# Reordering the attention steps of a fused attention and mixture-of-experts kernel

## Chip, cores and metric

One core of one Trainium2 chip. The metric is the device time of one execution in microseconds (us), as the median over runs. Engines are named as in the profile: PE is TensorE (PEld its weight load), DVE VectorE, ACT ScalarE, POOL GpSimd, SP SyncE, which here only issues DMAs.

## The reference, cut to what matters

```python
# x: (4, 512, 512); 16 heads of 32
h = layernorm(x)
q, k, v = split(h @ w_qkv)
q, k = layernorm_per_head(rope(q)), layernorm_per_head(rope(k))
a = tril((q @ k.T) ** 4)
x = x + ((a / a.sum(-1)) @ v) @ w_out
h = layernorm(x)
# 16 experts, 4 groups: the 2 best groups, in them the 4 best experts of each token,
# weights normalised and scaled by 2.5
x = x + sum_over_chosen(w_e * expert_e(h)) + shared_expert(h)
```

## The kernel before

Each engine has its own instruction stream, written out by hand, and semaphores between them. The part that the change touches is the attention of the four batches (`B = 4`, 512 tokens in `MB = 4` pieces of 128). A batch b is a sequence of 16 steps, `i = 4 m + p`: group m of four heads (`HG`), key piece p. Behind it come the projection with `w_out` and the residual (lines 559 and 1445), then the next batch. After the last batch come 96 expert tiles (some 590 us), which the change leaves alone.

A step has, on PE, `scores(b, i)` (L533: 12 matmuls in four banks, one for each head, the query width 512 - 128 p), then `fill`, then `values(b, i - 1)` (L548: 16 matmuls that add up values and row sums over the four key pieces of a group in banks 6 and 7), then `fill_behind`. The fills are work for the batch after (nb = b + 1), the one after that (lb = b + 2) and the one before (pb = b - 1), and they share two PSUM banks, bkA and bkB: q, k and v products of nb (L485, 8 matmuls for one of the three over one 128-token piece), transposes of its q and k (L494), of the first norm (L473) and of the second norm's rows (L473), the router's logits (L500), `places` (L510, L511) and `table` (L519).

ACT squares the scores of each head (`square`, L910), squares two of the four once more (`fourth`, L903; DVE does the other two in `fourths`, L1420), and splits a piece of an expert weight into two f16 parts (`split_next`, L819 and L821). POOL multiplies the diagonal block of each head by the causal mask (L1065) and computes the low f16 part (L1073). `scores(b, i + 1)` waits for the squares of step i, `values(b, i)` for the masks of step i, and the squares of step i + 1 for the second squares of step i.

- `finish(b, m)` on DVE (L1357 to L1363) reads banks 6 and 7 when the last `values` of group m is done, and divides. `values(b, 4 m + 4)`, the first of the next group, waits for it (`att_done`). Before, it stands ahead of the `fourths` of step 4 m + 5.
- `qkT` on ACT (L852, L856, two times each) empties both banks of q and k transposes, which PE writes at the end of steps 3, 7, 11 and 15. Before, the q half stands ahead of the next step's squares and the k half behind the second of them. PE's v product in the next step waits for the q half.
- `copy_v` (L878) empties the v product. Before, it stands at the start of step 4 m + 1, behind `split_next`. PE's q product of step 4 m + 1 waits for it. For batches from 2 on, its first one (m = 1, group step 4 or 5) also waits for `xn2_out`, the end of a 1 MB DMA that stores the second norm's rows of batch pb, because these rows lie in the same SBUF memory.
- `head_squares`, `head_variance`, `head_deviation`, `head_normed` (L882 ACT, L1403 DVE, L886 ACT, L1407 and L1411 DVE) are one chain for the norm of q and k; `centre` (L1393 to L1399, DVE) is ahead of it.
- SP issues in one queue: `store_half(n)` waits for the low part of piece n, which is done at the end of every second step; a store and a load of 768 KB follow. The row store (L380) waits for `xn16_ready`, which comes from `rows_lo` (L1425) in step 2, and stands behind the pieces of steps 1 and 3.
- Routing of batch pb on DVE, one serial chain of small operations: `group_sums`, `group_choice`, `compare`, `expert_choice` (which releases `places`), `choice_weights`, `choice_values`, `choice_places` (which releases the bank for the last q and k transposes), `place_rows` (L1328, L1329).

## Time and profile before

| | |
|---|---|
| median of 3 runs | 1217.14 us (1215.68 to 1225.99) |
| profiled execution | 1209.58 us, span 1207.6 us |
| mean granted TensorE clock | 0.905 of 2.4 GHz |
| busy share of the span | PE 79%, DVE 63%, ACT 47%, POOL 44% |
| attention steps of batches 0, 1, 2, 3 | 104.1, 134.6, 124.5, 94.9 us |

The difference between 1209.58 and 1207.6 us is what lies before the first and behind the last instruction. A timeline row has start, duration, engine, line, operation, what it writes and reads, how many instructions are merged in it, and in brackets how long its engine sat idle before it and which engine and line ended that. A group's duration is from the first start to the last end.

### The profile page before, as it was taken

The page shows a single profiled execution, that of the slowest core. Times are in us where ns is not written, and L with a number is a line of the kernel's source. Part 1 is how long each engine was busy: PE and PEld are TensorE (multiplying, and loading weights), DVE is VectorE, ACT ScalarE, POOL GpSimd, SP SyncE. Part 2 cuts the span into 40 slices and gives each one's busy share as a digit, 9 for nine tenths or more (in the row PEclk, how much of TensorE's full clock was granted, in tenths as well). Part 3 has the DMA queues.
Part 4 walks back from the last instruction along what each step waited for, and adds up shares of the span by engine and source line. Part 5 has one row for each costly group of instructions (what it writes and reads, how often), then busy time and mean ns, then how long its engine had stood idle before and what let it go on. Part 6 is the DMA issues. An engine that isn't in the chain of part 4 may idle for free. (4 is left out here: it accounts for less than half of the span.)

```text
span 1207.6 us, 21002 instructions
## 1 busy us (share of the span) xinstructions
PE 958.4 (79%) x5770; PEld 455.7 (38%) x5771; DVE 756.9 (63%) x1663; ACT 563.6 (47%) x1009; POOL 529.1 (44%) x738
## 2 busy tenths in 40 slices
PE   5967789869777785984777799888888798878883
PEld 2432333324333332341343454444344344434441
DVE  2857865867888588849648665554455544545552
ACT  2347874866537665577235234333333233333330
POOL 0005663544415545367302003555555555555553
PEclk9988999888879887976868899899999989999996
DMA  8002333433323333655346896777777777778874
GB/s 330 13 35 93 118 105 137 140 119 112 107 88 100 137 107 110 236 204 192 107 148 207 304 319 184 193 185 184 174 188 191 178 179 181 190 174 193 183 187 78
DMA packets 76648, 193.48 MB, mean 160 GB/s; under 512 B 9904, under 2 KB 11056, under 8 KB 75312
## 3 DMA queue, kind: packets, MB, share of 16 engines
q1 hardware_dynamic: 58672, 149.53, 35.9%
q0 software_dynamic: 17920, 43.26, 19.6%
q8 instruction: 28, 0.46, 0.1%
q14 instruction: 28, 0.23, 0.1%
HBM read 131.67 MB, written 61.10 MB: 160 GB/s over the span
## 5 line engine op out<-in xcount | busy, mean ns | idle before, releaser
L743 PE MATMUL bank<-arena,xgT 128*128 (+1 forms) x1152 | 288.0, 387 | 3.6 <-ACT xgT L1029 3.1
L1065 POOL TENSOR_TENSOR s_p<-s_p,c_causal 128x128 f32<-128x128 f32 x256 | 153.8, 624 | 304.3 <-DVE s_p L1420 282.7
L485 PE MATMUL bank<-arena 128*128 128x512 f32 x384 | 196.5, 663 | 43.8 <-ACT arena L856 14.6
L1022 ACT ACTIVATE hT<-bank 128x512 f16<-128x512 f16 x96 | 57.3, 597 | 273.1 <-PE bank L753 273.1
L743 PEld LDWEIGHTS bank<-arena,xgT 128*128 128x128 f16 x1152 | 109.2, 100 | 133.1 <-issue 45.4
L1073 POOL TENSOR_TENSOR arena<-arena 128x768 f16<-128x768 f32 x68 | 113.0, 1662 | 87.8 <-ACT arena L821 87.7
L1109 POOL DMA_INDIRECT out<-yy,sidx x80 | 128.6, 1608 | 46.1 <-issue 44.6
L764 PE MATMUL bank<-wd,hT 128*128 128x512 f16 x576 | 146.0, 391 | 0.7 <-ACT hT L1022 0.7
L910 ACT ACTIVATE arena<-bank 128x512 f32<-128x512 f32 (+3 forms) x256 | 100.8, 439 | 93.2 <-PE bank L533 92.6
L1694 DVE TENSOR_SCALAR yy<-bank,hsc 128x512 f32<-128x512 f32 x80 | 60.0, 750 | 122.8 <-DMA out<-yy,sidx 116.6
L1029 ACT ACTIVATE xgT<-bank 128x1024 f16<-128x1024 f16 x96 | 98.2, 1023 | 78.7 <-PE bank L734 77.4
L485 PEld LDWEIGHTS bank<-arena 128*128 128x128 f32 x384 | 78.3, 213 | 146.0 <-issue 93.0
L1420 DVE TENSOR_TENSOR s_p<-arena 128x512 f32<-128x512 f32 (+3 forms) x128 | 69.0, 558 | 73.5 <-ACT arena L910 72.3
L734 PE MATMUL bank<-ident,xg 128*128 128x128 f16 x768 | 61.1, 224 | 63.1 <-DMA xg<-xn_scratch,gidx 62.9
L1103 POOL DMA_INDIRECT xg<-xn_scratch,gidx x80 | 86.7, 1084 | 40.6 <-issue 39.1
L1654 DVE TENSOR_TENSOR hh<-sg,bank 128x256 f32<-128x256 f32 x96 | 40.4, 421 | 80.8 <-ACT sg L1038 79.5
L734 PEld LDWEIGHTS bank<-ident,xg 128*128 128x128 f16 x768 | 47.5, 100 | 102.5 <-DMA xg<-xn_scratch,gidx 94.6
L764 PEld LDWEIGHTS bank<-wd,hT 128*128 128x128 f16 x576 | 53.5, 100 | 49.6 <-issue 4.9
L1090 POOL COPY wr<-xg 128x1 f32 x80 | 60.2, 752 | 13.3 <-PE bank L734 10.3
L533 PE MATMUL bank<-arena 32*128 32x512 f16 (+3 forms) x768 | 50.1, 319 | 18.6 <-ACT arena L910 13.6
L548 PE MATMUL bank<-s_p,arena 128*32 128x512 f32 (+3 forms) x256 | 40.0, 523 | 28.9 <-DVE arena L1363 22.5
L903 ACT ACTIVATE s_p<-arena 128x512 f32<-128x512 f32 (+3 forms) x128 | 60.9, 476 | 2.0
(172 smaller groups left out, 1390.2 us busy)
## 6 DMA issues: line engine op xcount, KB each, us to landing
wd<-w_scratch SPq DMA_DIRECT2D x82, 512.0 KB, 4.2
arena<-w_experts SPq DMA_DIRECT2D x34, 768.0 KB, 6.0
w_scratch<-arena SPq DMA_DIRECT2D x34, 768.0 KB, 4.5
arena<-w_scratch SPq DMA_DIRECT2D x17, 1024.0 KB, 7.7
xin<-x SPq DMA_DIRECT2D x4, 1024.0 KB, 5.5
arena<-x SPq DMA_DIRECT2D x4, 1024.0 KB, 4.8
x_scratch<-arena SPq DMA_DIRECT2D x4, 1024.0 KB, 5.2
xg<-xn_scratch SPq DMA_DIRECT2D x16, 256.0 KB, 4.5
```

The lines of the kernel that those rows point to most:

```text
L485: mm = pe.matmul(bk[:], xnT[:, c, m * P:m * P + P], wqkv[:, c, w * E:w * E + E], start=(c == 0), stop=(c == EC - 1))
L734: mm = pe.transpose(oct16(bank[k])[:, c], xg[:, k, 0:E].bitcast(F16)[:, c * P:c * P + P], ident16[:])
L743: mm = pe.matmul(bank[2 + k][:], xgT[:, k, xh * EC + c, :], w, start=(c == 0 and xh + wh == 0), stop=(c == EC - 1 and xh == 1))
L764: mm = pe.matmul(bank[5 + k][:], hT[:, k, hh_ * FC + c, :], wd[:, k, wh, c, :], start=(c == 0 and hh_ + wh == 0), stop=(c == FC - 1 and hh ...
L903: act.activation(s_p4[:, i % 2, j, 0:w], s_sq[:, j, 0:w], ACT.Square).then_inc(p4_done[1], 1)
L910: act.activation(s_sq[:, j, 0:w], bank[j][:, 0:w], ACT.Square, scale=1.0 / (QS * QS)).then_inc(sq_done, 1)
L1029: act.activation(xgT[:, k], oct16(bank[k]), ACT.Copy).then_inc(gT_sb, 1)
L1065: pool.tensor_tensor(d, d, C["causal"][:], ALU.mult).then_inc(p4_masked, 1)
L1073: pool.tensor_tensor(halves[:, j, 1, a], stage[:, j, a], halves[:, j, 0, a], ALU.subtract).then_inc(lo_done, 1)
L1103: pool.indirect_dma_start(out=xg[:, k], out_offset=None, in_=xn_dram, in_offset=bass.IndirectOffsetOnAxis(ap=gidx[:, k:k + 1], axis=0)).th ...
L1109: pool.indirect_dma_start(out=out, out_offset=bass.IndirectOffsetOnAxis(ap=sidx[:, k:k + 1], axis=0), in_=yy[:, k], in_offset=None, comput ...
L1420: dve.tensor_tensor(s_p4[:, i % 2, j, 0:N - P * kb], s2, s2, ALU.mult).then_inc(p4_done[0], 1)
```

## The change

- PE: `values(b, i - 1)` goes ahead of `fill(b, i)` in the steps where i is 4, 8 or 12. In the last batch, the logits' 32 matmuls are spread over steps 5 and 6, two token pieces in each.
- DVE: `finish(b, m)` goes from ahead of the `fourths` of step 4 m + 5 to behind the `fourths` of step 4 m + 4, ahead of `split_qk`, `head_variance` and all else of that step. In the last batch likewise, and there `group_sums`, `group_choice` and `compare` each come one step later (7, 8 and 9, the last one together with `expert_choice`). In step 15, `choice_places` goes ahead of `centre`.
- ACT: all PSUM copies stand at the end of the step in which PE fills the bank, `qkT` in one piece there; `copy_v` of steps 4, 8 and 12 ahead of `split_next`, and `head_squares` from between the squares to behind `copy_v`. `copy_rows(3)` comes ahead of the first norm's activations in step 6. In the last batch `copy_logits` stands in step 7 instead of 6.
- SP: the row store stands behind one piece instead of two.

```diff
-                halves_of(b, 0, 2)
+                halves_of(b, 0, 1)
                 if b:
                     sp.wait_ge(xn16_ready, b)
                     sp.dma_start(xn_dram[N * (b - 1):N * b, 0:E]...).then_inc(xn2_out, 16)
-                halves_of(b, 2, 4)
+                halves_of(b, 1, 4)
...
-                elif i == 5:
-                    for m in range(MB):
+                elif i in (5, 6):
+                    pe.wait_ge(x2T_sb, upto(pb, 3))
+                    for m in (2 * i - 10, 2 * i - 9):
                         logits(pb, m, bkA)
...
                     scores(b, i)
+                    if i and i % MB == 0:
+                        values(b, i - 1)
                     if b + 1 < B:
                         fill(b, i)
-                    if i:
+                    if i % MB:
                         values(b, i - 1)
...
+            def behind(b, i):
+                nb, pb, lb, m, p = b + 1, b - 1, b + 2, i // MB, i % MB
+                if p == 3:
+                    qkT(nb, m, bkA, bkB)
+                elif i == 0 and b:
+                    copy_first(nb, 3, bkA)
+                elif i == 4 and b:
+                    copy_rows(pb, 1, bkB)
+                elif i == 5 and b:
+                    copy_rows(pb, 2, bkB)
+                elif i == 6 and b:
+                    copy_rows(pb, 3, bkA)
+                elif i == 8 and b:
+                    copy_logits(pb, bkB)
+                    gate_scores(pb)
+                elif i == 9:
                     copy_v(nb, 0, bkB)
...
-                    if nb < B and p == 0:
-                        if m:
-                            qkT(nb, m - 1, bkA, bkB, (1,))
-                        head_squares(nb, m)
                     square(b, i, 2)
                     fourth(b, i, 1)
                     square(b, i, 3)
                     fourth(b, i, 3)
+                    if nb < B and p == 0:
+                        if m:
+                            copy_v(nb, m, bkA)
+                        head_squares(nb, m)
                     if i == 2 and b:
                         rows_hi(b - 1)
                     split_next(b, i)
+                    if nb < B:
+                        behind(b, i)
...
-                if p == 1 and m:
-                    finish(b, m - 1)
-                elif p == 2 and (m < MB - 1 or lb < B):
+                if p == 2 and (m < MB - 1 or lb < B):
...
                 if p == 0:
                     if m:
+                        finish(b, m - 1)
                         split_qk(nb, m - 1)
                     head_variance(nb, m)
                 elif p == 1:
                     head_normed(nb, m)
-                elif p == 3 and (m < MB - 1 or lb < B):
+                if i == 15 and b:
+                    choice_places(pb, bkA)
+                if p == 3 and (m < MB - 1 or lb < B):
                     centre(nb if m < MB - 1 else lb, (m + 1) % MB)
...
-                        if i % MB == 1 and i > 1:
+                        fourths(b, i)
+                        if i and i % MB == 0:
                             finish(b, i // MB - 1)
-                        fourths(b, i)
                         last_behind(b, i)
```

## Rows read from the trace of the kernel before

**Rows 1.** Busy time by stretch: the 16 steps of batches 0 to 3.
```profile
core 0: us, PE busy (x) PEld busy (x) DVE busy (x) ACT busy (x) POOL busy (x), PEclk, DMA share, GB/s
88.91:192.99 104.08, 84.32 (x589) 33.87 (x589) 77.88 (x118) 80.80 (x162) 64.89 (x80) 0.93 0.31 107
...
206.92:341.51 134.59, 102.22 (x658) 45.46 (x657) 103.65 (x176) 89.78 (x177) 65.63 (x80) 0.84 0.36 123
...
356.32:480.83 124.51, 91.14 (x662) 41.59 (x661) 94.79 (x156) 85.12 (x169) 64.28 (x80) 0.86 0.34 115
...
495.95:590.84 94.89, 63.86 (x546) 27.99 (x545) 73.87 (x142) 67.39 (x141) 62.83 (x80) 0.77 0.58 206
```

**Rows 2.** Waits of PE in 88 to 592 us: total, times, longest.
```profile
PE bank L548 <- DVE arena L1363: 34.9, 6, 11.0
PE bank L485 <- ACT arena L856: 14.6, 7, 3.2
...
PE bank L485 <- ACT arena L878: 11.5, 6, 5.9
PE bank L485 <- ACT vtok L878: 9.2, 3, 7.9
PE bank L494 <- DVE rb L1295: 8.9, 2, 5.9
```

**Rows 3.** Timeline of PE in batch 2: steps 4, 5 and 13.
```profile
385.89 3.70 PE L485 MATMUL bank<-arena 128*128 128x512 f32 x8 [1.77 <-ACT arena L856]
...
397.26 5.71 PE L485 MATMUL bank<-arena 128*128 128x512 f32 x8 [5.91 <-ACT arena L878]
...
466.33 1.94 PE L548 MATMUL bank<-s_p,vtok 128*32 128x512 f32 x8 [10.97 <-DVE arena L1363]
```

**Rows 4.** Timeline of ACT: first value copy of batches 1 and 2.
```profile
247.36 0.60 ACT L878 ACTIVATE vtok<-bank 128x512 f32<-128x512 f32 x1 [5.71 <-DMA xn_scratch<-vtok]
...
396.61 0.60 ACT L878 ACTIVATE arena<-bank 128x512 f32<-128x512 f32 x1 [3.75 <-DMA xn_scratch<-arena]
```

**Rows 5.** Timeline of SP's queue in batch 1, the row store.
```profile
236.75 0.97 SPq L380 DMA_DIRECT2D xn_scratch<-vtok  x1
```

**Rows 6.** DMA issues in 200 to 600 us: KB each, median us to landing.
```profile
x_scratch<-arena SPq DMA_DIRECT2D x3, 1024.0 KB, 5.4
```

**Rows 7.** Timeline of DVE in batch 2: rows' low part, a finish, the ranks.
```profile
376.07 2.79 DVE L1425 SCALAR_TENSOR_TENSOR arena<-arena 128x512 f16<-128x512 f32 x4 [0.79 <-ACT arena L895]
...
393.10 0.70 DVE L1357 STREAM_TRANSPOSE arena<-bank 128x512 f32<-128x512 f32 x1
...
457.17 2.56 DVE L1219 TENSOR_TENSOR rb<-rb,c_tie 128x1024 f32<-128x1024 f32 x1
```

**Rows 8.** Timeline of ACT in batch 2, from the q and k copies to the split.
```profile
384.41 0.76 ACT L852 ACTIVATE arena<-bank,ln_b,ln_s 128x512 f16<-128x512 f32 x1
...
392.02 0.84 ACT L821 ACTIVATE arena<-arena 128x768 f32<-128x768 f32 x1
```

**Rows 9.** Timeline of POOL in batch 2, masks of step 3.
```profile
382.33 2.73 POOL L1065 TENSOR_TENSOR s_p<-s_p,c_causal 128x128 f32<-128x128 f32 x4 [1.39 <-DVE s_p L1420]
```

**Rows 10.** Timeline of DVE in batch 1, from step 10 to the finish.
```profile
290.69 0.76 DVE L1420 TENSOR_TENSOR s_p<-arena 128x256 f32<-128x256 f32 x2 [1.05 <-ACT arena L910]
...
341.64 0.72 DVE L1357 STREAM_TRANSPOSE arena<-bank 128x512 f32<-128x512 f32 x1 [1.36 <-PE bank L548]
```

**Rows 11.** Timeline of ACT in batch 0, step 0.
```profile
94.32 1.06 ACT L882 ACTIVATE arena<-arena 128x1024 f32<-128x1024 f32 x1 [3.47 <-DVE arena L1399]
```

**Rows 12.** Timeline of PE: first fill of batch 0, logits of batch 3.
```profile
97.99 5.17 PE L485 MATMUL bank<-arena 128*128 128x512 f32 x8
...
525.96 7.01 PE L500 MATMUL bank<-gwT,arena 128*128 128x16 f32 x32
```

**Rows 13.** Timeline of DVE: place_rows behind batch 2, and two rows of batch 3.
```profile
491.60 0.29 DVE L1328 TENSOR_SCALAR ra<-c_iota,kf 128x128 f16<-128x128 f32 x1
...
535.17 0.90 DVE L1420 TENSOR_TENSOR s_p<-arena 128x256 f32<-128x256 f32 x2 [10.43 <-ACT arena L910]
...
571.12 1.66 DVE L1328 TENSOR_SCALAR ra<-c_iota,kf 128x128 f16<-128x128 f32 x1
```

42 lines of the change are left out of this document (10 added, 32 removed).

## The prediction

> **What bounds the kernel now.** I read the busy time by stretch first. In the attention no engine is full: PE is busy 84.3 of 104.1 us in batch 0, 102.2 of 134.6, 91.1 of 124.5 and 63.9 of 94.9 us in batches 1 to 3, DVE 77.9, 103.7, 94.8 and 73.9 us [rows 1]. So these 458 us are chains and waits, and the granted clock there is 0.77 to 0.93. Next, PE's waits, since PE issues scores, fills and values in one fixed order and holds up everyone else [rows 2]: 34.9 us for `finish` in six places, 14.6 us for the q and k copies, 11.5 + 9.2 us for value and norm copies, 8.9 us for `choice_places`. These are 79 us. A wait that goes is worth only the distance to what is late next, so I followed each batch through its steps, with the durations of the trace and the new order; times below are on the clock of the trace before, each batch from its own start.
>
> **Row store.** It is issued at 236.75 us in batch 1 [rows 5], right behind the store and load of piece 1, and ACT waits for its end until 247.36, 5.71 us; in batch 2 it waits 3.75 us [rows 4]. Put behind one piece, it waits for `rows_lo` alone, which in batch 2 ends at 376.07 + 2.79 = 378.9 [rows 7]. A 1 MB store with nothing before it lands in 5.4 us by the median [rows 6]. So it ends near 384 to 385, and the new first `copy_v` comes at about 390: the wait goes, with 5 us in hand.
>
> **Step 4 of batch 2, as the pattern.** Before, ACT works from 384.41 without a break to 392.02 + 0.84 = 392.9 [rows 8]: four copies for q and k (2.6 us), four squares and two second squares, `head_squares` (1.0), split (1.7). `copy_v` comes after that. New: copies until 387.1, squares until 390.2, `copy_v` 390.8, `head_squares` 391.7, split 393.4. PE: the masks of step 3 end at 382.33 + 2.73 = 385.06 [rows 9]; the v product waited for ACT until 385.89 anyway [rows 3]. So `values(3)` (0.8 us) fits into that wait, moves out of the time behind the v product, and costs nothing. The v product ends at 389.6, scores of step 5 at 390.9, and the q product starts at 391.0 instead of 397.26. It also takes 3.7 instead of 5.71 us, if PE keeps the upper clock, since the 5.91 us pause before it is gone [rows 3]. `finish` starts on DVE right behind the second `fourths` at 389.4 instead of 393.10 [rows 7]; it takes 2.6 us and ends at 392.0, before PE asks for it at 394.7. Scores of step 6 start at 397.2 instead of 405.35 (8.1 us sooner).
>
> Late next: `copy_rows(2)` stands behind the split of step 5, which now ends at 399.1, since ACT waits about 0.3 us in `head_deviation` for `head_variance`, which DVE reaches only behind `finish` and `split_qk`. PE's k product waits for it, 2.1 us, and the gain is 6.3 us. It stays so through steps 8 and 9 (there 0.8 us for `values(7)` is won and the same is given back), and DVE's `group_choice` chain sets the q and k transposes of step 11 both before and after.
>
> **Second half of batches 1 and 2: DVE is the bound.** In batch 1 DVE works from 290.69 to the `finish` at 341.64 with five pauses, 1.01, 0.95 and 0.37 us between the two rows of 1.05 and 1.36 [rows 10]; behind it come `split_qk` and `place_rows`, which end 0.17 us before the first residual addition. So however much PE wins, this half shrinks by at most the pauses from the first row on, 1.0 + 0.95 + 0.4 + 1.4 = 3.7 us. The 5.18 us `finish` wait of step 13 in batch 1 and the 10.97 us of batch 2 [rows 3] go, because `finish` then precedes the ranks chain that starts at 457.17 [rows 7] and takes 6.5 us. But `values(13)` then waits for `fourths(13)`, which stands behind this chain. In batch 2 I get 462.8 for the end of these masks' values against 471.65, and with `choice_places` at 468.5 the projection starts at 471.7 instead of 480.83. In batch 1, `choice_places` ahead of `centre` takes the 5.9 us wait away [rows 2], but the sum of DVE's work then holds the residual: it wins 3.6 us, not 7.3.
>
> Sums: batch 2: 9.2 us (6.3 + 2.9). Batch 1: its first half wins 8.0 us up to step 6 (wait of 7.9 us with the store gone), then loses 1.5 us since `copy_rows(3)` now keeps the first norm's two activations (1.5 us) behind PE, ahead of the squares of step 7, and gets 0.4 back: 6.8, and 3.6 behind: 10.4 us.
>
> **Batch 0.** In step 0, ACT waited 3.47 us in `head_squares` for DVE's `centre`, with two squares behind it [rows 11]. New: they go first; ACT is ready 2.1 us sooner, the q fill of 97.99 starts at about 93.2, when the scores are done [rows 12]. 4.5 us is left at step 3. Step 4 adds as above up to 8, but DVE still has `first_norm_stats` (2.9 us) ahead of `fourths(5)`, and ACT's step 7 waits for its result: 5.3 left. Steps 9 and 12 give 6.6 to 8.9, and the end 6.7 us.
>
> **Batch 3.** No fills. `finish` already ran right behind `fourths` in step 5, as nothing stood between, so its first wait of 1.8 us stays. Spread over two steps, the logits (7.01 us at the lower clock [rows 12]) end at the same time, 536.5 by my count. But DVE, which sat idle 10.43 us until 535.17 and then works without a break up to the last `place_rows` [rows 13], starts `group_sums` only behind `fourths` of step 7, at 539.9 instead of 536.0. It had 1.8 us of `fourths` and 0.3 us of pauses in between: a loss of 1.9 us. PE waits at `places` until 560.5 instead of 558.3. The two long `finish` waits (6.93 and 8.59 us) are not worth their length, since DVE's chain is the bound and not PE.
>
> **Sum.** 6.7 + 10.4 + 9.2 - 1.9 = 24.4 us. The experts' part has no edit; I take it as it is. From the profiled execution: 1209.6 - 24.4 = 1185.2 us. This execution lies 7.6 us under the median of the runs, so the forecast for the median is 1217.1 - 24.4 = 1192.7, say 1193 us. Own range 1186 to 1201: each batch's sum is good to 2 us or so, by the spread of PE's eight-matmul products over 3.7 and 5.7 us.
>
> **Rival 1: PE runs the new order at the lower clock.** The v product is now preceded by scores, a pause and sixteen thin matmuls, and PE still pauses 0.5 to 2 us in places. Products took 5.2 to 5.7 us instead of 3.7 after such stretches [rows 3, 12]. If all nine v products and nine q products behind them lose half of that difference, (5.3 - 3.7) x 18 / 2 = 14 us, minus what the pauses before the next wait absorb (some 2 us): a gain of 12 us, 1205 us. Against it: in batch 2 the product at 385.89 ran in 3.70 us after 1.77 us of pause [rows 3]. The Trainium skill, TensorE: Matmul & The Clock Gate, section "A second HAM failure mode: psum-queue depth-cycling", says that short PE pauses between groups of matmuls can make the clock fall and rise again and again; by that rule this rival would be the case, and the row at 385.89 speaks against it.
>
> **Rival 2, slower: the norm chain holds ACT.** `copy_v` and `head_squares` now stand ahead of the split and of the next squares, and `head_variance` behind `finish` (2.6 us) and `split_qk` (1.8 us); `head_deviation` on ACT waits for it, with three squares of step 4 m + 1 behind it, thus PE's next scores, thus DVE. I count 0.3 to 2 us of wait in each of nine groups. If it is above 2.7 us in each (9 x 2.7 = 24.4), nothing is left; at 4 us it is 12 us slower, 1229 us. A v product at the lower clock (1.6 us later) and DVE's own `first_norm_stats` would bring it there. Against it: `split_next` (1.7 us) stands between and covers most.
>
> **Rival 3: the order does little,** because in each half another engine is at its bound, as DVE in rows 10: only the store's 9.5 us [rows 4] less the 1.9 us of batch 3 are won: 1209 us.
>
> **Rival 4: more.** Without the long pauses the granted clock in the attention rises from 0.77 to 0.93 [rows 1] to near 1, the products at 5.2 to 5.7 us take 3.7. Seven more of them than I counted, and the slow values and logits of batch 3, are 12 us: 1181 us.
>
> **A cost left out.** DVE and POOL slow each other: `ra` of `place_rows` takes 0.29 us behind batch 2 with POOL idle, and up to 1.66 us in batch 3 with POOL at work [rows 13]. A tighter order has more of this overlap. The Trainium skill, GPSIMD Engine Reference, section "Specifications", has the two engines share their SBUF interfaces, with contention where DVE has two SBUF inputs; the rows agree in kind, though `ra` has one such input. I take 0 for it and up to 4 us for the range (three long ones of 1.4 us).
>
> **Chances.** Forecast 0.62, rival 1 0.16, rival 2 0.06, rival 3 0.07, rival 4 0.09. The range takes in the forecast's own, rival 4's and rival 1's with a few us: 1179 to 1210. What a measurement can tell from no change is about 1%, 12 us: faster by more than that 0.82, within it 0.12, slower 0.06.
>
> **What would show it.** PE's waits for L1363 fall from 34.9 to under 12 us, those of the first half of batches 1 and 2 for L878 to under 1 us each; the row store is issued near step 3's start and lands in 5 to 7 us; ACT shows no wait for a DMA; batches 0 to 3 take about 97, 124, 115 and 97 us; in batch 1 the projection ends before DVE and the residual waits for `place_rows`; in step 15 the transposes come before `centre`. I would be wrong if ACT waits over 2 us in `head_deviation` in most groups, or if the v products run over 5 us.

## The result and the profile after

Median 1172.6 us (1169.13 to 1174.09, 4 runs) against 1216.89 us; the ratio is 0.9624 (95%: 0.959 to 0.9658), 44.3 us faster. The forecast was 1193 us with a range down to 1179: the sign was right, the size was not. The profiled execution of the changed kernel took 1174.09 us, its span is 1172.1 us. One profile below, that of a_both_early, is of an execution slower than the others of its kernel (1190.1 us against 1172.3 to 1185.5), and its batches are not used.

The busy time of the changed kernel by stretch, the 16 steps of batches 0 to 3, answers to [rows 1]; its batch 3 is cut where the projection starts (before, that point is 98.25 us behind batch 3's first scores):

```profile
core 0: us, PE busy (x) PEld busy (x) DVE busy (x) ACT busy (x) POOL busy (x), PEclk, DMA share, GB/s
88.64:182.97 94.33, 87.79 (x589) 35.11 (x589) 79.89 (x118) 80.66 (x162) 63.30 (x80) 0.96 0.34 118
196.90:311.60 114.70, 97.74 (x657) 44.38 (x656) 97.97 (x171) 89.64 (x177) 64.33 (x80) 0.94 0.39 134
328.80:444.43 115.63, 95.60 (x660) 42.91 (x660) 94.67 (x157) 84.45 (x168) 62.61 (x80) 0.88 0.36 124
458.72:551.93 93.21, 67.57 (x577) 30.05 (x577) 73.62 (x147) 67.61 (x141) 62.83 (x80) 0.84 0.61 221
```

The whole attention (first scores of batch 0 to the start of the last projection) went from 505.3 to 463.3 us, 42.0 us less. The experts' part took 620.1 us against 613.4 without an edit; it wanders by more than 10 us from one execution to the next (604 to 624 us over all runs below), so experiments are read first by their attention, batch by batch.

PE's waits of the changed kernel in 88 to 560 us, in total, times and longest, against [rows 2] (L1367 is `finish`, L875 `copy_first`, L1069 the masks):

```profile
PE bank L548 <- POOL s_p L1069: 14.1, 16, 4.6
PE bank L548 <- DVE arena L1367: 10.3, 4, 4.7
PE bank L533 <- ACT arena L913: 9.1, 19, 0.9
PE bank L485 <- ACT arena L875: 8.7, 4, 3.0
PE bank L494 <- DVE rb L1299: 5.7, 2, 4.2
```

The long waits are gone: `finish` fell from 34.9 us in six places to 10.3 in four, the 14.6 us for the q and k copies are no longer among the first rows. What leads now is a wait for POOL's masks. Steps 4 and 5 of batch 2, the worked pattern of the prediction, on PE and ACT, and SP's row store in batch 1, against [rows 3 to 5, 8]:

```profile
360.03 3.70 PE L485 MATMUL bank<-arena 128*128 128x512 f32 x8 [0.15 <-ACT arena L859]
...
364.98 3.70 PE L485 MATMUL bank<-arena 128*128 128x512 f32 x8 [0.21 <-ACT arena L881]
```

```profile
364.35 0.58 ACT L881 ACTIVATE arena<-bank 128x512 f32<-128x512 f32 x1
364.82 1.05 ACT L885 ACTIVATE arena<-arena 128x1024 f32<-128x1024 f32 x1
...
368.37 0.32 ACT L889 ACTIVATE hs<-hs,eps 128x32 f32<-128x32 f32 x1
```

```profile
219.95 0.39 SPq L380 DMA_DIRECT2D xn_scratch<-vtok  x1
```

The q product follows the v product by 4.95 us instead of 11.37 and takes 3.70 us instead of 5.71. `copy_v` shows no bracket: it waits for nothing, the DMA included. The row store lands 4.2 us behind its issue in batches 1 and 2 (10.5 and 8.2 us before), sooner than the 5 to 7 us foretold. `head_deviation` (L889) waits here for nothing; over the attention it waits 3.8 us in five places, 1.0 us at the longest, so the slower rival did not happen.

### The profile page after: what moved, and what is told of

The parts are those of the page before. It is cut to its first block and busy times, and to the rows that moved or that the text cites. A ratio compares the mean times of both kernels' runs of the same rounds, so it can differ in the third digit from the quotient of the medians.

```text
span 1172.1 us, 21004 instructions
## 1 busy us (share of the span) xinstructions
PE 964.3 (82%) x5770; PEld 457.7 (39%) x5771; DVE 752.5 (64%) x1663; ACT 563.5 (48%) x1009; POOL 524.0 (45%) x738
## 5 line engine op out<-in xcount | busy, mean ns | idle before, releaser
L1069 POOL TENSOR_TENSOR s_p<-s_p,c_causal 128x128 f32<-128x128 f32 x256 | 148.5, 605 | 256.2 <-DVE s_p L1424 249.6
L485 PE MATMUL bank<-arena 128*128 128x512 f32 x384 | 187.8, 638 | 18.3 <-ACT arena L875 9.4
L1113 POOL DMA_INDIRECT out<-yy,sidx x80 | 128.4, 1605 | 46.1 <-issue 43.2
L485 PEld LDWEIGHTS bank<-arena 128*128 128x128 f32 x384 | 74.9, 204 | 112.7 <-issue 91.6
L1424 DVE TENSOR_TENSOR s_p<-arena 128x512 f32<-128x512 f32 (+3 forms) x128 | 73.6, 602 | 43.3 <-ACT arena L913 41.3
L533 PE MATMUL bank<-arena 32*128 32x512 f16 (+3 forms) x768 | 54.1, 323 | 16.2 <-ACT arena L913 9.1
L1094 POOL COPY wr<-xg 128x1 f32 x80 | 60.0, 750 | 13.3 <-PE bank L737 10.3
L1103 POOL COPY sidx<-row_id 128x1 int32 (+1 forms) x80 | 14.7, 183 | 102.4 <-DMA out<-yy,sidx 90.0
```

What stands on the lines that cost most here:

```text
L485: mm = pe.matmul(bk[:], xnT[:, c, m * P:m * P + P], wqkv[:, c, w * E:w * E + E], start=(c == 0), stop=(c == EC - 1))
L1069: pool.tensor_tensor(d, d, C["causal"][:], ALU.mult).then_inc(p4_masked, 1)
L1113: pool.indirect_dma_start(out=out, out_offset=bass.IndirectOffsetOnAxis(ap=sidx[:, k:k + 1], axis=0), in_=yy[:, k], in_offset=None, comput ...
L1424: dve.tensor_tensor(s_p4[:, i % 2, j, 0:N - P * kb], s2, s2, ALU.mult).then_inc(p4_done[0], 1)
```

## The experiments

Times of the attention, in us, from each kernel's trace: batches 0 to 2 from their first scores to the next batch's, batch 3 to its projection; then the median of all its timed runs and the ratio to the kernel before on the same chip (one chip runs that kernel in 1204 us instead of 1215 to 1219, so medians of different calls are not compared).

| kernel | b0 | b1 | b2 | b3 | sum | median | ratio (95%) |
|---|---|---|---|---|---|---|---|
| before | 118.0 | 149.4 | 139.6 | 98.3 | 505.3 | 1216.9 | |
| after | 108.3 | 131.9 | 129.9 | 93.2 | 463.3 | 1172.6 | 0.962 (0.959 to 0.966) |
| after_again | 108.3 | 132.0 | 130.3 | 98.3 | 468.9 | 1171.9 | 0.965 (0.961 to 0.969) |
| a_store_late | 108.2 | 139.0 | 136.4 | 92.9 | 476.5 | 1188.1 | 0.976 (0.971 to 0.981) |
| a_values_late | 113.5 | 139.9 | 134.1 | 95.4 | 482.9 | 1192.1 | 0.981 (0.975 to 0.986) |
| a_copies_late | 122.4 | 136.7 | 134.4 | 92.9 | 486.5 | 1197.2 | 0.983 (0.978 to 0.988) |
| b_store | 121.1 | 141.8 | 133.3 | 98.1 | 494.3 | 1207.3 | 0.993 (0.990 to 0.997) |
| b_values | 120.1 | 143.6 | 134.7 | 97.5 | 495.9 | 1209.8 | 0.993 (0.989 to 0.997) |
| b_copies | 113.4 | 150.2 | 140.6 | 95.3 | 499.5 | 1210.5 | 0.995 (0.991 to 0.998) |
| a_last_old | 108.3 | 133.7 | 129.9 | 96.5 | 468.3 | 1175.2 | 0.966 (0.962 to 0.970) |
| a_last_busy | 108.3 | 133.2 | 128.8 | 95.9 | 466.2 | 1162.6 | 0.967 (0.964 to 0.969) |
| a_busy | 108.3 | 132.0 | 130.3 | 97.0 | 467.5 | 1166.7 | 0.968 (0.964 to 0.972) |
| b_busy | 117.7 | 148.9 | 139.8 | 99.4 | 505.7 | 1204.4 | 1.000 (0.998 to 1.002) |
| a_norm_first | 108.3 | 134.8 | 132.9 | 97.0 | 473.0 | 1182.2 | 0.975 (0.967 to 0.982) |
| a_head_early | 108.3 | 132.2 | 129.6 | 93.2 | 463.2 | 1173.0 | 0.965 (0.959 to 0.971) |
| a_choice_later | 108.3 | 133.2 | 127.9 | 96.1 | 465.5 | 1171.3 | 0.975 (0.972 to 0.977) |
| a_first_early | 108.3 | 133.4 | 133.0 | 93.2 | 467.9 | 1179.2 | 0.971 (0.967 to 0.975) |
| a_both_early | 108.4 | 133.4 | 135.2 | 97.5 | 474.4 | 1177.2 | 0.969 (0.964 to 0.974) |
| b_narrow | 118.0 | 139.4 | 134.7 | 83.7 | 475.9 | 1181.7 | 0.971 (0.965 to 0.976) |
| a_narrow | 107.8 | 123.8 | 121.2 | 88.0 | 440.9 | 1146.2 | 0.942 (0.936 to 0.947) |

The names with a are the changed kernel with something more, those with b the kernel before.

How far a batch wanders by itself can be read from batches that no edit of a run touches. With the changed order, batch 0 is the same to 0.1 us in eight executions, batch 1 takes 131.9 to 133.7 us (after, after_again, a_busy, a_last_busy, a_last_old) and batch 2 128.8 to 132.9 us (the same and a_norm_first); with the order before, batch 0 takes 117.7 to 121.1 us (before, b_busy, b_store). The q product of batch 2's step 9 takes 3.70 us in one of these executions and up to 6.2 us in another, and the like holds for others. So a difference of this size between two profiles is not the price of an edit, unless it arises in the step where the edit acts.

### One part taken out, and one part alone

**The row store** put back in the changed kernel, and moved alone in the kernel before (the same two lines, the other way round):

```diff
-                halves_of(b, 0, 1)
+                halves_of(b, 0, 2)
...
-                halves_of(b, 1, 4)
+                halves_of(b, 2, 4)
```

> The changed kernel with the row store back behind the second half of the pieces (halves_of(b, 0, 2)). ACT's copy_v of block 1 stands in step 4 and waits for this store's end. In the kernel before it waited 5.71 and 3.75 us in batches 1 and 2 (9.5 in all), but there copy_v came some 5 us later in the step order than it does now. Theory A (one chain, the waits are in series): the wait is back with that distance on top, 10 us in each of the two batches, so 18 to 20 us slower than the changed kernel (about 1192 us), all of it in steps 4 and 5 of batches 1 and 2. Rival (something else is late there too, such as copy_rows or finish): at most the 9.5 us or less come back, about 1180 us.

> The kernel before with the row store behind one piece of the halves, nothing else. Theory A (waits in series, worth less alone than together, 13.2 us being its price in the changed kernel's attention): here copy_v comes later in the step order, so only the 5.71 + 3.75 = 9.5 us that ACT waited can go; PE's pauses of 7.9 and 5.9 us ahead of the q product fall to the 2.1 us of the other groups. 8 to 10 us faster than before, in steps 4 and 5 of batches 1 and 2. Rival (the price of the store is the same with either order): 13 us faster, for instance because the q product then also runs in 3.7 instead of 5.7 us.

The timeline of ACT in a_store_late shows the wait back, and longer than in [rows 4], as `copy_v` asks sooner now:

```profile
236.12 0.60 ACT L881 ACTIVATE vtok<-bank 128x512 f32<-128x512 f32 x1 [7.73 <-DMA xn_scratch<-vtok]
...
378.32 0.60 ACT L881 ACTIVATE arena<-bank 128x512 f32<-128x512 f32 x1 [6.37 <-DMA xn_scratch<-arena]
```

14.1 us of wait, and 13.5 us more in batches 1 and 2: the chain of Theory A, with the distance put 4 to 6 us too long. Alone the store wins 7.6 + 6.3 us there. Of these, 6.2 + 4.1 = 10.3 us are won by the scores of step 6, right behind the wait, near the 9.5 us that ACT waited [rows 4]; the rest comes in steps 8 and 9, where two products took 3.70 instead of 5.31 and 5.40 us. In batch 0, which the edit does not touch, two others took 5.40 instead of 3.70 us, and the batch is 3.1 us longer. The timed gain is 8.4 us. So Theory A is nearer, and whether the rest belongs to the store these runs do not show.

**Values and finish** of the group end, out of the changed kernel and alone (PE and DVE as in the diff ahead of the prediction, nothing else):

> The changed kernel with PE's values of a group's last step again behind the v product, and with DVE's finish again in the next step ahead of the second fourths (in batch 3 too). Theory A (each part only exposes the next wait, so a part taken out costs more than its share): PE's waits for finish come back to near 30 us from 10.3, and the kernel is 15 to 22 us slower, about 1190 us; the v and q products behind the waits fall to the lower clock again (5.3 to 5.7 us). Rival 1 (the copies of ACT were the main part; v product starts early anyhow): under 8 us slower, about 1179 us. Rival 2 (DVE is the bound in the second halves whatever PE does): the loss is in the first halves alone, about 10 us, 1183 us.

> The kernel before with the values of a group's last step ahead of the v product, and finish behind the second fourths one step sooner; ACT's order, the store and batch 3's logits as before. Theory A (the prediction's slower rival is real when this part stands alone: finish and split_qk, 4.5 us, come ahead of head_variance, and ACT waits for that in head_deviation with copy_v and three squares behind it, 2.9 us in each group of batch 0 of the run without the new copies): batch 0 takes 107 to 109 us instead of 104.1, the other batches win little, and the whole is 0 to 6 us faster or slower than before, about 1215 us. Rival (parts add up, 44 us in all less 13 for the store and less 23 for the copies): 8 us faster or more in the attention, spread over all batches, batch 0 shorter than 104 us.

Out: 19.6 us in the attention, 5.3 in batch 0, 8.0, 4.2 and 2.2 in the others, so Theory A holds in its size and neither rival does. PE's waits for `finish` in a_values_late are

```profile
PE bank L548 <- DVE arena L1365: 43.3, 9, 10.9
```

more than the kernel before had in all (34.9). Alone: batch 0 is 2.1 us longer than before, less than batch 0 wanders in this order, but the ACT waits of b_values in batch 0 are such as Theory A had:

```profile
ACT hs L888 <- DVE hs L1405: 8.2, 3, 2.9
```

This is the wait of the prediction's slower rival, 2.7 us in each of three groups: with ACT's old order `copy_v` stands behind it. In the changed kernel, where `copy_v` stands ahead, the same wait is 1.0 us at the longest. The three other batches win 5.8, 4.9 and 0.8 us, mid-way between Theory A and the rival.

**ACT's copies**, out and alone:

> The changed kernel with ACT's order of the kernel before: the PSUM copies (q and k, v, rows, logits, first blocks) at the head of the next step or the one after it, head_squares behind the second square. Theory A (chain): the v product waits for the q and k copies again (14.6 us in all before), and copy_v stands one step later, so that the q product waits for it; 15 to 20 us slower, about 1190 us. Rival 1 (the gain came from values and finish): under 8 us slower. Rival 2 (with values first, PE has other work while the copies run, as values(3) lies ahead of the v product now): about 8 to 10 us slower, since 0.8 us of each wait is covered and the rest is not; 1182 us.

> The kernel before with ACT's order of the changed kernel alone (PSUM copies in the step that filled the bank, copy_v and head_squares behind the squares). Theory A (parts need one another; the copies are the largest one, 23.2 us in the attention when taken out): batch 0 at about 99.6 us, as when only values and finish were taken out of the changed kernel; batches 1 and 2 win by copy_v coming sooner but still wait for the store; 12 to 16 us in the attention. Rival (they add up): 44 less 13 for the store and 20 for values and finish, 9 to 11 us.

Out: 23.2 us, and 14.2 of them in batch 0, which is then 4.4 us slower than in the kernel before; the same 8.2 us of `head_deviation` waits stand in its trace. Theory A held, a little above its 20. Alone: batch 0 wins 4.6 us as expected, batches 1 and 2 lose 0.8 and 1.0, and the attention wins 5.8 us, so the 12 to 16 us were wrong, and the rival's 9 to 11 too. In b_copies ACT arrives sooner at the same DMA and waits longer than in [rows 4]:

```profile
243.27 0.60 ACT L878 ACTIVATE vtok<-bank 128x512 f32<-128x512 f32 x1 [7.92 <-DMA xn_scratch<-vtok]
...
397.39 0.60 ACT L878 ACTIVATE arena<-bank 128x512 f32<-128x512 f32 x1 [6.40 <-DMA xn_scratch<-arena]
```

Together: in batches 0 to 2 (407.0 us before, 370.1 after) the three alone win 10.8 + 8.6 + 2.9 = 22.3 us (25.4 without the 3.1 us of b_store's untouched batch 0), the three taken out cost 13.5 + 17.4 + 23.4 = 54.3 us, and the change is 36.9 us. It is one chain with several waits in each step; a wait removed alone mostly shows the next one.

### Batch 3: order or clock

The forecast had a loss of 1.9 us there, the profile a gain of 5.0. Undone alone: logits all in step 5, copied in step 6, `group_sums` in step 6.

> The changed kernel with batch 3's logits all in step 5 again, their copy in step 6, and group_sums on DVE in step 6 (values and finish as in the changed kernel). Theory A (the prediction's step was right in its mechanism, the spread delays group_sums by one step): batch 3's steps are 2 to 4 us shorter than the 89.8 us of the changed kernel, about 1170 us. Rival 1 (the clock): eight small matmuls in a row behind a pause fall to the lower level and take 7 us instead of 2 x 1.96 us, so that group_sums starts no sooner; batch 3 takes 89 to 91 us, no change. Rival 2 (the spread itself won the 5 us of batch 3): batch 3 back at 94 to 95 us, about 1177 us.

Batch 3 took 96.5 us, between the theories. The added matmuls were to settle it, here in PE's steps of batch 3 (4, 4, 12 and 16 in steps 3, 5, 9 and 13 of b_busy; 4, 4, 2 and 8 in a_busy; only the first two in a_last_busy):

```diff
+            def busy(n):
+                for _ in range(n):
+                    pe.matmul(bkA[:], ones[:], wout[:, 0, :], start=True, stop=True)
```

> The kernel before with matmuls of 128x512 added in batch 3 alone, whose results are overwritten (ones by wout into the logits' bank): 4 in step 3 ahead of the third transposes, 4, 12 and 16 of them where PE waits for finish in steps 5, 9 and 13 (waits of 1.8, 6.9 and 8.6 us; one such matmul takes 0.46 us at the upper clock, and none of them is to outlast its wait). Nothing else of the order is changed, so this run moves TensorE's clock alone. Theory A (batch 3's time hangs on the granted clock, 0.77 there, lower level in 25 to 42 us from its start, under the logits, which take 7.0 us): clock above 0.9, logits 4 us instead of 7, group_sums 2 to 3 us sooner, batch 3's steps 94 to 95.5 us instead of 98.25. Rival (DVE's chain is the bound and the clock is only PE's): the logits are quicker but batch 3 stays at 97.5 to 98.5 us, or the added work makes it longer.

> The changed kernel with batch 3's logits in one block in step 5 and group_sums in step 6 (as in the run of that alone, whose batch 3 took 96.5 us with the clock at its lower level from 25 to 42 us), plus the 4 + 4 added matmuls of steps 3 and 5. Theory A (the clock, not the spread of the logits over two steps, makes the 3.3 us between that run and the changed kernel): logits in about 4 us, batch 3 at 92 to 93.5 us. Theory B (the spread itself is what wins, since scores of step 6 come between the two halves): batch 3 at 95.5 us or more though the logits run at the upper clock.

> The changed kernel with added matmuls in batch 3: 4 in step 3, 4, 2 and 8 in steps 5, 9 and 13. In the changed kernel's profile batch 3 has a granted clock of 0.84 and takes 93.2 us. Theory A (the clock is worth something in every order, about 2 us in this batch): 91 to 92 us. Rival (with the logits at the upper clock already, the rest hides behind DVE's chain): 93 us as it is.

All three came out against Theory A, but none is a clean test: in each, the four matmuls of step 3 outlast the wait that they were to fill, and the scores of step 4 come 3.5 us later. In b_busy the clock of batch 3 rose from 0.77 to 0.95 and the logits took 4.0 us instead of 7.0, yet `group_sums` began only 1.3 us sooner, DVE then paused 2.5 us behind step 13, where it had not paused before, and the batch took 99.4 us. In a_last_busy the logits took 4.88 us, between the two levels. What settled it was the changed kernel run again:

> The changed kernel once more, on the chip of the next three, for comparison on one chip. Theory A (batch 3's form is set by the order ahead of it, since the first steps of batches 0 to 3 came out alike to 0.1 us in kernels that agree up to there): batch 3 at 93 us again, with the logits in 2 x 1.96 us and group_sums at 38.7 us. Rival (it is chance from one execution to the next): batch 3 at 96 to 97 us with the logits at the lower clock and group_sums at 42 to 43 us.

Its batches 0 to 2 repeat to 0.4 us; batch 3 took 98.3 instead of 93.2 us. The logits (L500) of the first and of the second execution, on PE:

```profile
489.24 1.96 PE L500 MATMUL bank<-gwT,arena 128*128 128x16 f32 x16
...
493.00 1.96 PE L500 MATMUL bank<-gwT,arena 128*128 128x16 f32 x16
```

```profile
490.54 3.60 PE L500 MATMUL bank<-gwT,arena 128*128 128x16 f32 x16
...
497.55 3.60 PE L500 MATMUL bank<-gwT,arena 128*128 128x16 f32 x16
```

and the stretches around them, first and second execution; the third number from the end is the granted clock:

```profile
489.00:495.50 6.50, 6.50 (x84) 4.79 (x84) 0.85 (x2) 4.60 (x11) 4.70 (x9) 1.00 0.43 131
```

```profile
490.00:502.00 12.00, 12.00 (x84) 8.37 (x84) 0.85 (x2) 5.12 (x11) 6.14 (x9) 0.50 0.39 133
```

The same 84 matmuls fill 6.5 us at 2.4 GHz and 12.0 at 1.2 GHz. So `group_sums` starts 38.9 us behind the batch's first scores in one and 44.1 us in the other; 44.0 is what the prediction had worked out (539.9 us on the clock of the trace before). From there to the projection it is 54.3 and 54.2 us, 58.2 in the kernel before. Over the kernels with the changed order the time of batch 3 is these two numbers added: 53.8 to 54.3 us where the logits are spread and `finish` is in its new place, 56.2 or 56.4 with the old logits (`fourths` of step 7 inside the chain), 56.7 with the old `finish`; and a start at 38.7 to 38.9 us where all spread logits ran at the upper clock, 41.9 to 44.1 where they or a part did not, 42.7 with the added matmuls of a_busy. The rival of after_again's expectation held; its batch 3 was even longer than the 96 to 97 us expected.

### Single places

**The first norm**, its second half in step 7, ahead of the q and k copies, as in the kernel before. (The expectation says that the prediction had it there; the prediction names only the half in step 6, of which more below.)

```diff
                     split_next(b, i)
+                    if i == 7 and lb < B:
+                        first_norm(lb + 1, (2, 3))
                     if nb < B:
                         behind(b, i)
```

> The changed kernel with the second half of the first norm (two activations, 1.5 us) in step 7 ahead of the q and k copies, which is where the prediction had it. Theory A (the prediction lost 1.3 us in batch 0 and 1.5 to 2 us in batch 1 at this place): the v product of step 8 starts 1.5 us later, batches 0 and 1 are 1.3 to 2 us longer each (95.8 and 116.5 us), about 3 us in all, 1176 us. Rival (PE has values(7), 0.8 us, and scores to do and hides it): under 1 us in all.

Batch 0 is the same to 0.1 us, batch 1 is 2.9 us longer (with its projection), and 2.7 of them stand at the scores of step 9, right behind the edit, where the other kernels agree to 0.4 us: Theory A and the rival each hold in one batch. The v and q products of steps 8 and 9 of batch 1, in the changed kernel and in a_norm_first:

```profile
249.81 3.70 PE L485 MATMUL bank<-arena 128*128 128x512 f32 x8 [0.16 <-ACT arena L859]
...
258.11 4.68 PE L485 MATMUL bank<-arena 128*128 128x512 f32 x8
```

```profile
251.78 5.10 PE L485 MATMUL bank<-arena 128*128 128x512 f32 x8 [1.56 <-ACT arena L859]
...
260.89 5.40 PE L485 MATMUL bank<-arena 128*128 128x512 f32 x8
```

1.4 us more of pause came with 1.4 us more of the v product behind it: the price of the wait was doubled by the clock. The 0.7 us of the q product is not clear of chance, since with the same order up to there it took 4.7 to 6.1 us. Batches 2 and 3, which the edit does not touch, were 2.9 and 3.8 us longer too; for batch 3 that is its lower-clock form, with `group_sums` at 43.2 us.

**head_squares** of step 0 between the squares again (batches 1 and 2):

> The changed kernel with head_squares of step 0 of batches 1 and 2 between the squares as before, as t1 has been centred since the batch before. Theory A (its new place behind the squares makes head_variance, head_deviation and the copies of step 1 late; PE's wait ahead of the q product of step 1 grew from 1.6 to 3.0 and 2.6 us): batches 1 and 2 are each 1 to 1.6 us shorter (113.4 and 114.3 us), 1170 us. Rival (the two squares behind it come 1 us later, and DVE and PE with them; what is won in step 1 is lost in step 0): within 0.5 us of the changed kernel in each batch.

The rival, by the end of the batch: 132.2 and 129.6 against 131.9 and 129.9 us. But not by its mechanism: in batch 1 the scores of steps 4 to 10 come 1.0 to 1.2 us sooner, as Theory A had it, and that is gone at steps 12 and 13, in the half where DVE works without a pause.

**expert_choice** one step later (`elif i == 13` for `i == 12`):

> The changed kernel with expert_choice behind the second fourths of step 13 instead of step 12. In batch 2 of the changed kernel PE waits 4.6 us for the masks of step 13, since their fourths stand behind expert_choice and the ranks. Theory A (DVE's work is the sum that counts in this half): the wait of 4.6 us goes but comes back at places, as choice_weights ends at the same time; within 1 us per batch. Rival 1 (PE is the bound): 2 to 4 us shorter in batches 1 and 2 each. Rival 2 (the choice becomes late and choice_places holds the transposes of step 15): 1 to 3 us longer each.

Batch 1 loses 1.3 us, and 1.2 of them appear between the scores of steps 14 and 15, where the edit acts. Batch 2 is 2.0 us shorter, but 3.0 us of lead stand already at step 10, ahead of the edit: the q product of step 9 took 3.70 us instead of 5.82. In a_last_busy, whose batch 2 is untouched, the same product took 3.70 us too, and the batch is 1.1 us shorter. The wait of 4.6 us for the masks of step 13 is no longer among PE's longest, but for the edit this leaves 0.8 us. So none of the three holds for both batches, and what bounds batch 2 this run does not show. Timed on one chip, the kernel is no gain: its ratio is 0.975 (0.972 to 0.977), that of a_busy and a_last_busy 0.968 and 0.967.

**copy_first sooner**, and with the later choice in batch 2:

```diff
                         if m:
                             copy_v(nb, m, bkA)
+                        elif b:
+                            copy_first(nb, 3, bkA)
                         head_squares(nb, m)
...
+                    if i == 13 and lb < B:
+                        copy_first(lb, 2, bkB)
                     split_next(b, i)
```

> The changed kernel with copy_first of step 0 (batches 1 and 2) right behind the squares, ahead of head_squares and of the two split copies (1.7 us), and that of step 13 ahead of the split. PE's waits for L875 are 8.7 us there in four places, 3.0 and 2.6 us ahead of the q product of step 1 and 2.6 us ahead of the k product of step 14. Theory A (the wait in step 1 is on the path, as PE, ACT and DVE are all behind it): batches 1 and 2 are each 2 to 3 us shorter than in the changed kernel (112 and 113 us), with step 14 hidden behind DVE; 4 to 6 us in all. Rival 1 (head_squares and head_variance become later by 0.5 us and take it back): 1 us or less per batch. Rival 2 (another phase of the clock takes more than it gives): longer.

> The same with expert_choice in batch 2 behind the second fourths of step 13 (alone it made batch 2's steps 2.2 us shorter, 113.45 against 115.63 us, and batch 1's 1.3 us longer, so it stays in step 12 there). Theory A (they add up): 2 us less than the kernel with the copies alone, all in batch 2. Rival (the sum of DVE's work, or batch 3's form at the lower clock, gives it back): no difference or up to 3 us longer, in batch 3.

This was the try at a version that beats both, and neither is faster than the changed kernel on the same chip (1179.2 and 1177.2 against 1171.9 us). The intervals of the ratios overlap. In the trace of a_first_early the scores of step 2 come 4.4 and 3.2 us sooner in batches 1 and 2, but those of step 4 come 0.4 and 3.2 us later. The further 1.1 us by which batch 1 is longer comes in its second half, as it did in a_last_busy without an edit. The q and k products of steps 1 and 2 of batch 2, in the changed kernel and in a_first_early, on PE:

```profile
337.49 5.95 PE L485 MATMUL bank<-arena 128*128 128x512 f32 x8 [2.56 <-ACT arena L875]
...
349.48 3.70 PE L485 MATMUL bank<-arena 128*128 128x512 f32 x8 [1.85 <-DVE slot_tab L1340]
```

```profile
337.59 5.35 PE L485 MATMUL bank<-arena 128*128 128x512 f32 x8
...
352.62 6.36 PE L485 MATMUL bank<-arena 128*128 128x512 f32 x8 [5.49 <-DVE slot_tab L1340]
```

The wait for `copy_first` is gone from the first product. The second waits for DVE's table (L1340) whatever ACT does; from the batch's start it begins at 20.7 and at 21.2 us. The 2.56 us only moved into the pause ahead of it, and it then took 6.36 instead of 3.70 us. Rival 2 held in batch 2. A wait was removed ahead of another one and the clock charged for it. Of the later choice on top (a_both_early), 2.0 us in the median are inside the spread, so its theory and its rival stay undecided.

### What POOL costs DVE

Left over was some 2.5 us of DVE's own instructions in the second half of batch 1 (the expectations have 2.6). In both kernels POOL's low halves of the expert weights were cut to 32 of 768 columns a piece (the rest left out, as zeros), with all waits kept:

```diff
+                a = slice(q * PIECE, q * PIECE + 32)
                 pool.tensor_tensor(halves[:, j, 1, a], stage[:, j, a], halves[:, j, 0, a], ALU.subtract
```

> The kernel before with POOL's low halves of the expert weights (split_lo) computed for 32 of 768 columns in each piece, all waits as they were, so that POOL is nearly idle beside its masks; the low halves of the weights are otherwise left out (zeros), so the experts' result is less exact. Theory A (DVE's small instructions of 1.2 to 1.7 us instead of 0.2 are contention with POOL): these are gone, DVE's time from the fourths of step 10 to the last residual addition in batch 1 falls from 66.4 to below 62 us, batch 3's chain from group_sums to the end (58.5 us) to about 54 us. Rival (they come from something else, as the queue of DVE itself): 66 and 58 us as before.

> The changed kernel with the same cut in split_lo. Theory A (the changed kernel has less of this contention by chance of the places, 2.6 us in the second half of batch 1 and 2 us in batch 3): DVE from the fourths of step 10 to the residual in batch 1 falls from 60.3 us by only half of what the kernel before gains, and the difference between the two kernels in this stretch is 3.5 to 4 us (the pauses alone) instead of 6.1. Rival (contention is the same in both): the difference stays near 6 us.

Groups of DVE in the kernel before and in b_narrow over the attention: count, then busy us and mean ns of one, then idle before.

```profile
L1397 DVE TENSOR_SCALAR hs<-hs 128x32 f32<-128x32 f32 x12 | 15.7, 1305 | 0.9
L1328 DVE TENSOR_SCALAR ra<-c_iota,kf 128x128 f16<-128x128 f32 x48 | 20.9, 436 | 0.0
L1219 DVE TENSOR_TENSOR rb<-rb,c_tie 128x64 f32<-128x64 f32 (+1 forms) x6 | 7.6, 1270 | 0.2
```

```profile
L1400 DVE TENSOR_SCALAR hs<-hs 128x32 f32<-128x32 f32 x12 | 2.2, 182 | 0.9
L1331 DVE TENSOR_SCALAR ra<-c_iota,kf 128x128 f16<-128x128 f32 x48 | 15.0, 312 | 0.0
L1222 DVE TENSOR_TENSOR rb<-rb,c_tie 128x64 f32<-128x64 f32 (+1 forms) x6 | 4.9, 819 | 0.2
```

and POOL's low halves in the same two kernels:

```profile
L1073 POOL TENSOR_TENSOR arena<-arena 128x768 f16<-128x768 f32 x64 | 105.9, 1654 | 24.1 <-ACT arena L821 24.0
```

```profile
L1076 POOL TENSOR_TENSOR arena<-arena 128x32 f16<-128x32 f32 x64 | 16.1, 252 | 30.9 <-ACT arena L821 30.9
```

POOL's 90 us less make DVE's busy time 341.0 us instead of 388.2 and the attention 29.4 us shorter (28.0 from the changed kernel's second execution, 22.4 from its first). Part of that can be POOL's own: its masks stand behind the low halves, and PE's waits for them fell from 14.1 to 7.0 us between after and a_narrow; the runs do not separate the two. The scaling of 32 numbers a row took 1305 ns in the mean of twelve and takes 182. One of the twelve in the kernel before, with what POOL does beside it:

```profile
114.52 1.41 DVE L1397 TENSOR_SCALAR hs<-hs 128x32 f32<-128x32 f32 x1
```

```profile
114.25 1.64 POOL L1073 TENSOR_TENSOR arena<-arena 128x768 f16<-128x768 f32 x1
```

It ends at 115.93 us, 0.04 us behind POOL's piece. This is so in eleven of the twelve; the other one, at 92.81 us, has no work of POOL beside it and takes 0.18 us. Theory A of b_narrow holds for what the long ones are, and batch 3's chain fell further than it had: from 58.2 to 46.7 us instead of about 54. DVE's stretch in batch 1 fell from 66.4 to 59.5 us before and from 60.3 to 54.3 after, so the difference is still 5.2 us, of which pauses are 3.6, between the 3.5 to 4 and the 6 of a_narrow's two theories. Contention explains at most about 1 us of the 2.5, and even that is not clear of chance, since the stretch takes 60.3, 60.4, 60.9 and 61.7 us in after, a_busy, a_last_old and a_last_busy, whose batch 1 is alike. The Trainium skill, GPSIMD Engine Reference, section "Specifications", speaks of contention with DVE instructions in a 2-port perf mode or with two SBUF inputs. The row has one such input, so it could only be the first; in which mode it ran no view here shows.

## Why the prediction was wrong

| batch | forecast | first execution | second |
|---|---|---|---|
| 0 | 6.7 | 9.8 | 9.7 |
| 1 | 10.4 | 17.5 | 17.4 |
| 2 | 9.2 | 9.7 | 9.4 |
| 3 | -1.9 | 5.0 | 0.0 |
| attention | 24.4 | 42.0 | 36.4 |

**What held.** The method: PE's waits fell as foretold, the row store's wait left ACT, ACT waited at most 1.0 us in `head_deviation`, DVE's pauses bounded the second half of batch 1 (all four of them, 3.7 us, are gone), and its residual waited for `place_rows`. The first norm held too: "then loses 1.5 us since `copy_rows(3)` now keeps the first norm's two activations (1.5 us) behind PE, ahead of the squares of step 7". Batch 1's scores come 10.0 us sooner at step 6 and 8.5 us at steps 7 and 8. The rows of ACT in step 6 of the changed kernel:

```profile
243.61 0.60 ACT L840 ACTIVATE arena<-bank 128x512 f32<-128x512 f32 x1 [2.18 <-PE bank L473]
244.10 1.51 ACT L869 ACTIVATE xin<-xin,first 128x512 f32<-128x512 f32 x2
```

Batch 2 is right to 0.5 us in its sum, and in part by luck. Its steps 4 and 5 won 8.4 us for the 8.1 worked out. But steps 1 to 3 lost 1.6 us that the prediction did not have (PE's wait for `copy_first` in step 1 grew from 1.6 to 2.6 us, the product behind it from 5.21 to 5.95), the lead at step 10 is 4.9 us for 6.3, and the rest of the batch won 4.9 us for 2.9.

**The step that failed, first: the level of PE's products.** The prediction says of a product that it falls to 3.7 us only in the pattern of batch 2. In batch 1 it had 8.0 us at step 6 for a wait of 7.9 us, which leaves nothing for the product behind that wait, and 0.4 us for steps 8 and 9. These products, of steps 5, 8 and 9, in the kernel before

```profile
248.01 5.25 PE L485 MATMUL bank<-arena 128*128 128x512 f32 x8 [7.91 <-ACT vtok L878]
...
268.37 5.31 PE L485 MATMUL bank<-arena 128*128 128x512 f32 x8 [3.19 <-ACT arena L856]
...
278.45 5.38 PE L485 MATMUL bank<-arena 128*128 128x512 f32 x8
```

take 3.70, 3.70 and 4.68 us in the changed one. The last two stand above (at 249.81 and 258.11 us), the first is

```profile
229.52 3.70 PE L485 MATMUL bank<-arena 128*128 128x512 f32 x8
```

These are 1.6 + 1.6 + 0.7 = 3.9 of the 4.2 us by which batch 1's first half passed the forecast (11.0 against 6.8 us at the scores of step 10). In batch 0 the v product of step 8 went from 5.40 to 3.70 us, 1.7 of the 3.0 us there. Over the attention, 10 of 34 such products took more than 4.5 us before and 5 after, and what they took above 3.70 us fell from 17.4 to 8.9 us. It was Rival 4, which I gave 0.09, for whole batches at once; it holds in single products.

For the v product of step 8, a part of the change lies behind this that the prediction does not name: the second half of the first norm stood ahead of the q and k copies in step 7, and the diff puts it behind them, so that product no longer waits for it. With it put back (a_norm_first), the lead of batch 1 at step 10 is 8.1 us, 0.4 less than at step 8, where the prediction had 0.4 more. In batch 0 it costs nothing.

**Second, batch 3's DVE chain.** The start of `group_sums`, 44.0 us, was right for the lower clock and came so in the second execution; the first had the upper clock, which is worth 5.1 us. What was mis-sized is the chain behind it: I took 2.1 us out of it for `fourths`, and it is 3.9 to 4.0 us shorter. The 2.1 us are right (56.4 against 54.3 us, a_last_old). The old `finish` put back makes it 56.7 us, and the prediction had that edit at nothing in this batch; by what way `finish` shortens the chain is not shown.

**Third, batch 1's second half**, 6.5 us for 3.6: the bound counted DVE's pauses and took its instructions as fixed, and they took some 2.5 us less. At most about 1 us of that is contention with POOL, and part of it can be chance; the rest is open, as are 1.3 us of batch 0.

**The median.** The gain timed is 44.3 and 43.5 us, 2 to 7 above the attention's in the profiles. The experts' part has no edit, and the profiled execution before lay 7.6 us under its median; which part of it that was cannot be seen without a trace of each run. The range was too narrow below: its lower end was Rival 4's alone, and that the three misses could add up had no chance of its own. The parts tried alone do not show them: they sum to 22.3 us in batches 0 to 2, where I had 26.3.

Rival 1 had the clock lower in the new order; it rose (0.93 to 0.96, 0.84 to 0.94, 0.86 to 0.88 in batches 0 to 2). The rule that the prediction took from the Trainium skill, TensorE: Matmul & The Clock Gate, section "A second HAM failure mode: psum-queue depth-cycling", is not refuted by that: products of 4.1 to 6.8 us stand beside others of the same shape at 3.70 in every trace here. But it says nothing of which order has fewer, and here that was the tighter one (5 against 10).

## What to carry to other kernels

In a chain of four engines with several waits in each step, neither one part alone nor one part taken out prices a change: here they gave 22 and 54 us for a change of 37, and `values` and `finish`, which alone won 8.6 us, cost 17.4 when taken out. Follow each instruction of the new order in its place in the file, and write down for each wait what stands ahead of it; two activations that the prediction did not follow were worth 3 us. Before a difference between two profiles is called the price of an edit, look at which step it starts in, and at the batches that the edit does not touch. And a wait removed just ahead of another that stays is worth nothing, or less, if the pause then falls where the clock drops.

## What the runs showed of the hardware

- One kernel has two forms of a batch: 93.2 and 98.3 us, same order, the clock at 1.00 or 0.50 over the same 84 matmuls. In these two executions the sum of the other batches repeats to 0.5 us, but over the kernels with the changed order a batch 1 that no edit touched ranges over 1.7 us and such a batch 2 over 4.1 us. A profile of one execution cannot price an edit of under 5 us in such a batch by the batch's time alone.
- Matmuls added in pauses raised the clock of a batch from 0.77 to 0.95 and won nothing (ratio 1.000, 0.998 to 1.002): four of them cost 3.5 us, and of what was won in the logits DVE gave back 2.4 us in the chain behind them.
- DVE's smallest instructions pay most for POOL's work: 1.41 us against 0.18 for 32 numbers a row, since the instruction ended 0.04 us behind POOL's piece of 1.64 us whenever the two overlapped. The low halves on POOL, for which no wait of another engine is put down in the trace, cost the attention 22 to 29 us, and leaving most of them out is worth 37.7 us before (1181.7 against 1219.4 us) and gives 1146.2 us with the change, more than any other single part tried here. Such a kernel lacks work that the result needs, so this is a bound for moving it; where else it could go was not tried.
